# Cross-attention and sparse FFN: normed attention tiles without the turn back, with reciprocal norms spread over channels by DMA

## The reference, cut to what matters

```
def attention(q, k, v, ...):             # q = layernorm(x); k = v = ctx; per batch 64 channels x 512 positions
    qh, kh, vh = (W @ t split into 8 heads of 64 for W, t in ...)
    qh = softmax(qh, axis=channel) * SCALE;  kh = softmax(kh, axis=position)
    context = einsum('bhdn,bhen->bhde', kh, vh)
    out = einsum('bhde,bhdn->bhen', context, qh)          # then Wo @ out + bo: b x 64 x 512
    norm = max(sqrt(sum(out * out, axis=channel)), 1e-12) # one norm for each batch and position
    return out / norm * g * sqrt(64)

def ffn(x, c1_w, c2_w, w1, w2t):         # rows of 512, 1,792 = 56 blocks of 32 inner units
    idx = argmax of (x @ c1_w.T @ c2_w.T) in each block   # one unit in each block survives
    h = relu(w1[idx] . x);   return h @ w2t[idx]

x = x + attention(layernorm(x), ctx, ctx, ...)            # x, ctx: 32 x 64 x 512 float32
x = x + ffn(layernorm(x), ...)
```

## Time and profile before

| | |
|---|---|
| median of 3 runs | 748.57 us (748.07 to 752.73) |
| profiled execution | 750.29 us, of which the span 748.2 us |
| mean granted TensorE clock | 0.995 of full |
| DVE busy | 622.1 us (83%) |
| ACT busy | 400.9 us (54%) |
| POOL busy | 481.9 us (64%) |

### The profile page before, as it was taken

How to read it: one execution, slowest core, us unless ns; L and a number is a source line. 1 busy time by engine, 2 the same in 40 slices (tenths; PEclk the granted TensorE clock), 3 DMA queues, 4 the chain that set the end, 5 groups by cost and what they waited for, 6 DMA issues and landing times.

```text
span 748.2 us, 14582 instructions
## 1 busy us (share of the span) xinstructions
PE 737.2 (99%) x5210; PEld 563.3 (75%) x5210; DVE 622.1 (83%) x910; ACT 400.9 (54%) x773; POOL 481.9 (64%) x517
## 2 busy tenths in 40 slices
PE   8999999999999999999998999999999999999998
PEld 6566566566566566575667989898898989989896
DVE  6999999999999999999977677787877878777652
ACT  5899999999999999999830211111111111111110
POOL 2889999999988888687566263644535355263420
PEclk9999999999999999999998999999999999999999
DMA  6233434434433333231212113130130302111011
GB/s 169 71 85 101 127 103 107 126 98 113 120 91 89 96 93 91 71 86 43 78 29 64 38 24 105 21 106 20 25 105 20 106 19 75 52 24 50 20 52 34
DMA packets 66376, 55.23 MB, mean 74 GB/s; under 512 B 40704, under 2 KB 49536, under 8 KB 66304
## 3 DMA queue, kind: packets, MB, share of 16 engines
q1 hardware_dynamic: 65568, 53.44, 26.7%
q10 hardware_dynamic: 736, 0.85, 0.5%
HBM read 38.52 MB, written 8.39 MB: 63 GB/s over the span
## 4 chain that ended last, share of the span: by engine, by line
PE 90%; POOL 3%; SPq 2%; DVE 2%; ACT 2%; issue 1%; DMA 1%; POOLq 0%; DVEq 0%
PE slot L1106 20%; PE po L1234 14%; PE po L1124 11%; PE turn L1124 11%; PE turn L1219 8%; PE turn L1202 7%; PE slot L1260 6%; PE slot L1274 6%; PE po L1245 2%; SPq L275 2%; PE slot L1088 2%; POOL Q L532 2%; PE turn L1056 1%; PE turn L1065 1%; PE turn L1076 1%
## 5 line engine op out<-in xcount | busy, mean ns | idle before, releaser
L532 POOL TENSOR_TENSOR Q<-Q,qrec 128x1024 f32<-128x1024 f32 x64 | 121.2, 1905 | 33.8 <-DVE qrec L770 33.8
L422 POOL TENSOR_TENSOR E<-E,rank 128x512 bf16<-128x512 bf16 (+1 forms) x64 | 71.0, 1110 | 110.8 <-DVE E L618 109.8
L1237 PE MATMUL po<-QT,G 128*64 128x512 f32 x256 | 116.9, 599 | 0.0
L1234 PE MATMUL po<-E,ctxT 128*64 128x512 f32 x256 | 116.9, 599 | 0.0
L936 ACT ACTIVATE E<-slot,neg_kmax 128x512 f32<-128x512 f32 x128 | 86.4, 686 | 10.4 <-DVE neg_kmax L756 10.2
L722 DVE TENSOR_REDUCE qmax<-slot 128x16 f32<-128x1024 f32 x64 | 75.3, 1217 | 12.5 <-PE slot L1274 12.5
L1234 PEld LDWEIGHTS po<-E,ctxT 128*64 128x64 f32 x256 | 32.3, 136 | 65.0 <-issue 57.6
L435 POOL TENSOR_TENSOR behind<-E,first 128x512 bf16<-128x512 bf16 (+1 forms) x64 | 60.3, 943 | 31.7 <-DVE first L626 31.5
L762 DVE TENSOR_REDUCE qsum<-Q 128x16 f32<-128x1024 f32 x64 | 77.2, 1207 | 1.6 <-ACT Q L925 1.6
L756 DVE TENSOR_REDUCE neg_kmax<-slot 128x2 f32<-128x1024 f32 x64 | 76.3, 1193 | 0.6 <-PE slot L1260 0.2
L944 ACT ACTIVATE E<-turn 128x512 f32<-128x512 f32 x128 | 75.1, 613 | 3.1 <-PE turn L1202 2.1
(11 more groups left out here) (184 smaller groups left out, 1956.8 us busy)
## 6 DMA issues: line engine op xcount, KB each, us to landing
c_in<-in_ctx SPq DMA_DIRECT2D x64, 128.0 KB, 2.7
x_in<-in_x SPq DMA_DIRECT2D x64, 128.0 KB, 2.6
stage<-in_ffn_w SPq DMA_DIRECT2D x32, 225.0 KB, 2.6
out<-E SPq DMA_DIRECT2D x16, 256.0 KB, 2.3
ctxT<-in_ctxT SPq DMA_DIRECT2D x31, 128.0 KB, 2.1
attn_out<-po_sb SPq DMA_DIRECT2D x31, 128.0 KB, 2.3
attn<-attn_out SPq DMA_DIRECT2D x9, 256.0 KB, 3.7
E<-attn_out SPq DMA_DIRECT2D x7, 256.0 KB, 4.3
```

The lines of the kernel that those rows point to most:

```text
L532: nc.gpsimd.tensor_tensor(half, half, qrec[1 - par][:, s, :].unsqueeze(2).broadcast_to([P, HALF, D]), ALU.mult).then_inc(q_scaled, 1)
L1234: nc.tensor.matmul(po[0:C, :], ctxT[1 - par][:, m, :], E[1 - par][:, :, m * P:(m + 1) * P], start=(m == 0), stop=(m == NT - 1)).then_inc(p ...
L1237: nc.tensor.matmul(po[C:P, :], G[:, m, :], QT[m][:], start=(m == 0), stop=(m == HT - 1)).then_inc(out_mm, 1)
```

## The change

The attention tile is turned as before, but only to get the norms. ACT squares it in place in PSUM (`square`), and DVE's `norms` sums there. POOL inverts the norms of a pair of tiles in one pow over 16 columns (8 for tiles 0 and 1). PE turns these columns into rows: one transpose, `turn_factors`, in place of eight. ACT copies the 16 rows of 128 to SBUF (`keep_rows`), stores them to a new DRAM tensor `factors`, waits, and loads each batch's 512 factors back over 64 partitions (`exchange`: one store, four loads, on ACT's own queue; for tiles 0 and 1 on SP's). `scale` then multiplies the unturned tile by the spread factors, both in SBUF, and `residual` reads the tile from SBUF and not from a PSUM bank.

Orders change on every engine. `turn_attn`, `square` and `norms` of a pair stand one duo earlier (behind `down(d, 3)`); `turn_factors` stands behind `hide(d, 1)`. For tiles 0 and 1 norms sit in steps 24 and 27, scale (POOL) and residual in 26 and 29, moments in 28 and 30, and normalize is POOL's. SP loads the second attention tile of a pair after `added` and not after `attn_turned`.

```diff
+TURNS = (B - 8, B - 5)
...
-        norm, inv = ([sb(f"{n}{i}", [P, 2 * NT]) for i in range(2)] for n in ("norm", "inv"))
+        inv_rows = sb("inv_rows", [4 * NT, P])
+        norm, inv = (sb(n, [P, 2, 2 * NT]) for n in ("norm", "inv"))
...
-        attn = [attn0, E[0][:, 0, :]]
-        x2 = [x20, stage[1][:], E[0][:, 2, :], E[0][:, 3, :], po_sb[0][:], po_sb[1][:]]
-        works, turned_attns = [stage[0][:], work1[:]], [x_in[0][:], E[0][:, 1, :]]
-        attn_of = lambda a: attn0 if a < 2 else attn[a % 2]
-        work_of = lambda a: works[0] if a < 2 else works[a % 2]
-        square_of = lambda a: stage[1][:] if a == 1 else work_of(a)
-        turned_of = lambda a: (stage[1][:], attn0)[a] if a < 2 else turned_attns[a % 2]
+        attn = [stage[1][:], E[0][:, 0, :]]
+        x2 = [x20, attn0, E[0][:, 2, :], E[0][:, 3, :], po_sb[0][:], po_sb[1][:]]
+        works = [stage[0][:], work1[:]]
+        attn_of = lambda a: (attn0, stage[0][:])[a] if a < 2 else attn[a % 2]
+        work_of = lambda a: (stage[1][:], stage[0][:])[a] if a < 2 else works[a % 2]
+        spread_of = lambda a: (stage[1][:], attn0)[a] if a < 2 else (x_in[0][:], E[0][:, 1, :])[a % 2]
...
+        over_channels = lambda a, b: factors[a, b:b + 1].broadcast_to([C, N])
+        rows_of = lambda f: f.rearrange("b (t n) -> (b t) n", n=P)
+        by_pair = lambda ap: ap.rearrange("p (t b c) -> p t b c", b=2, c=C)
+        by_factor = lambda ap: ap.rearrange("p (b t) -> p t b", b=2)
+        inverted = lambda a: a + 1 if a < 2 else 2 + a // 2
...
+                def store_factor(a):
+                    sp.wait_ge(rows_kept, a + 1)
+                    sp.dma_start(rows_of(factors[a]), inv_rows[0:2 * NT, :]).then_inc(first_stored, 16)
+
+                def load_factor(a):
+                    sp.wait_ge(first_stored, 16 * (a + 1))
+                    for b in range(2):
+                        sp.dma_start(spread_of(a)[b * C:(b + 1) * C, :], over_channels(a, b)).then_inc(spread_in[a], 16)
...
-                    if known == 24:
+                    if known == TURNS[0] - 2:
...
-                            sp.wait_ge(attn_turned, a - 1)
+                            sp.wait_ge(added, a - 1)
...
+                def normalize(a):
+                    pool.wait_ge(x2_rstd, a + 1)
+                    nc.gpsimd.tensor_scalar(work_of(a), x2[a % 6], moments2[a][:, 0:1], rstd2[a][:], ALU.subtract,
+                                            ALU.mult).then_inc(x2_normed, 1)
+
+                def invert(a, w):
+                    pool.wait_ge(norm_max, a + w)
+                    if a > 1:
+                        pool.wait_ge(inv_turned, a // 2 + 1)
+                    nc.gpsimd.tensor_tensor(inv[:, a % 2:a % 2 + w], norm[:, a % 2:a % 2 + w],
+                                            neg_half[:].unsqueeze(2).broadcast_to([P, w, 2 * NT]),
                                             ALU.pow).then_inc(norm_inv, 1)
 
-                def scale_kept(a):
-                    pool.wait_ge(norm_inv, a + 1)
-                    pool.wait_ge(attn_kept, a + 1)
-                    nc.gpsimd.tensor_tensor(by_batch(turned_of(a)), by_batch(turned_of(a)),
-                                            inv[a % 2][:].unsqueeze(2).broadcast_to([P, 2 * NT, C]),
-                                            ALU.mult).then_inc(scaled, 1)
+                def scale(a):
+                    pool.wait_ge(spread_in[a], 32)
+                    nc.gpsimd.tensor_tensor(attn_of(a), attn_of(a), spread_of(a), ALU.mult).then_inc(scaled, 1)
...
-                    rank_mask(d, 3)
-                    select(d, 2)
-                    rank_mask(d, 4)
                     select(d, 3)
                     if not last:
-                        invert(2 * d + 2)
+                        invert(2 * d + 2, 2)
...
                     rank_mask(d, 0)
                     rank_mask(d, 1)
                     select(d, 0)
+                    rank_mask(d, 2)
                     select(d, 1)
-                    rank_mask(d, 2)
+                    rank_mask(d, 3)
+                    select(d, 2)
+                    rank_mask(d, 4)
...
-                def norms(a):
+                def norms(a, bank):
                     t = a % 2
                     dve.wait_ge(squared, a + 1)
                     if later(a - 1):
-                        dve.wait_ge(norm_inv, a - 1)
-                    nc.vector.tensor_reduce(norm[t][:], by_batch(square_of(a)), AX.X, ALU.add).then_inc(norm_sum, 1)
+                        dve.wait_ge(norm_inv, inverted(a - 2))
+                    nc.vector.tensor_reduce(by_factor(norm[:, t]), by_pair(bank[:]), AX.X, ALU.add).then_inc(norm_sum, 1)
                     dve.wait_ge(norm_sum, a + 1)
-                    nc.vector.tensor_scalar(norm[t][:], norm[t][:], NORM_EPS * NORM_EPS, None, ALU.max).then_inc(norm_max, 1)
+                    nc.vector.tensor_scalar(norm[:, t], norm[:, t], NORM_EPS * NORM_EPS, None, ALU.max).then_inc(norm_max, 1)
 
                 def scale(a):
-                    t = a % 2
-                    dve.wait_ge(norm_inv, a + 1)
-                    dve.wait_ge(attn_back, max(a - 1, 2))
-                    nc.vector.tensor_tensor(by_batch(turned_of(a)), by_batch(pre[t][:]),
-                                            inv[t][:].unsqueeze(2).broadcast_to([P, 2 * NT, C]), ALU.mult).then_inc(scaled, 1)
-
-                def residual(a, bank):
-                    t, r = a % 2, x2[a % 6]
-                    dve.wait_ge(attn_back, a + 1)
+                    dve.wait_ge(spread_in[a % 2], 32 * (a // 2 + 1))
+                    nc.vector.tensor_tensor(attn_of(a), attn_of(a), spread_of(a), ALU.mult).then_inc(scaled, 1)
+
+                def residual(a):
+                    r = x2[a % 6]
+                    dve.wait_ge(scaled, a + 1)
                     dve.wait_ge(gain_done, 1)
                     dve.wait_ge(xr_loaded[a % 4], 16 * (a // 4 + 1))
-                    nc.vector.scalar_tensor_tensor(r, bank[:], gain8[:, 0:1], r, ALU.mult, ALU.add).then_inc(added, 1)
+                    nc.vector.scalar_tensor_tensor(r, attn_of(a), gain8[:, 0:1], r, ALU.mult, ALU.add).then_inc(added, 1)
+
+                def moments_of(a):
...
+                    if later(q - 1):
+                        dve.wait_ge(hT_lo_done, q - 1)
...
-                    if d:
-                        first_max(d, 3)
+                    first_max(d, 3)
                     h_low(d, 0)
-                    if not last:
-                        norms(a)
                     first_max(d, 4)
                     block_max(d, 5)
-                    if not last:
-                        norms(a + 1)
-                        scale(a)
                     first_max(d, 5)
                     if d:
                         result_of(2 * d - 2)
                         result_of(2 * d - 1)
                     gate(d, 1)
-                    if not last:
-                        scale(a + 1)
                     block_max(d, 6)
                     h_low(d, 1)
-                    if not last:
-                        residual(a, pre[0])
                     gate(d, 2)
+                    if not last:
+                        for t in range(2):
+                            scale(a + t)
+                            residual(a + t)
+                            moments_of(a + t)
+                        normalize(a)
                     first_max(d, 6)
                     if not last:
-                        residual(a + 1, pre[1])
-                    h_low(d, 2)
+                        normalize(a + 1)
                     block_max(d, 7)
-                    if not last:
-                        normalize(a)
-                        normalize(a + 1)
-                    first_max(d, 7)
                     if not last:
                         xT_rest(a, pre[0])
                         xT_rest(a + 1, pre[1])
+                    h_low(d, 2)
+                    first_max(d, 7)
                     gate(d, 3)
+                    gate(d, 4)
+                    if not last:
+                        z_low(d + 1)
                     h_low(d, 3)
-                    gate(d, 4)
-                    if not last:
-                        z_low(d + 1)
-                    h_low(d, 4)
                     if not last:
                         block_max(d + 1, 0)
                         block_max(d + 1, 1)
                         first_max(d + 1, 0)
+                    h_low(d, 4)
+                    if not last:
                         block_max(d + 1, 2)
                         first_max(d + 1, 1)
+                        block_max(d + 1, 3)
                     gate(d, 5)
+                    if not last:
+                        first_max(d + 1, 2)
+                    gate(d, 6)
+                    if not last:
+                        block_max(d + 1, 4)
+                    if d + 2 < DUOS:
+                        norms(a + 2, pre[0])
                     h_low(d, 5)
```

(51 more changed lines are left out.)

126 lines of the change are left out of this document (62 added, 64 removed).

## The result

The changed kernel takes 743.69 us (median of 6 runs, 743.16 to 745.32) against 749.10 us for the kernel before (6 runs, 748.07 to 752.73): a ratio of 0.9926, 95% interval 0.9909 to 0.9942. Another five runs of it beside eleven of the kernel before gave 743.71 against 749.47, ratio 0.9929 (0.9917 to 0.9941). So it is faster, by 5.4 to 5.8 us or 0.7%: within 1%, inside the range of 738.5 to 748.0, and some 2.7 us above the 741.0 of the forecast. The profiled execution took 745.32 us with a span of 743.5 (before: 750.29 and 748.2).

What follows compares the result with a forecast made beforehand. TensorE (PE), busy 99% of the span, was taken as the bound; 4.0 (duos) + 2.8 (first duo) + 0.8 (attention) = 7.6 us gave 741.0 us. Summed terms ranged 739.0 to 743.5, the stated range 738.5 to 748.0.

Steps and rivals of the forecast that it cites:

- Part 1: Duos 1 to 6: eight transposes off PE, one added, net 0.67 us per duo, 4.0 us in all.
- The slack of 0.8 on DVE's chain: In each duo normalize(a+1) ends at 20.0 and PE wants it at 20.8 us, so PE need not wait.
- The first rival: Factors arrive late, so scale, DVE's queue and PE wait in each duo; up to 754 us, chance 0.12.
- the second, the port: DVE waits for POOL's SBUF port, four instructions a duo, each up to 0.65 us longer; taken at 747, chance 0.10.
- Part 2: First duo: PE leaves turn_x(3) at 409.2 instead of 411.98, gain 2.8 us.
- The stop at turn_factors: First duo: PE waits 2.1 us for POOL's power of sixteen columns, or 0.9 if it costs as little as eight.
- shorter than the 2.54 after which the clock was seen to fall: First duo: the new 2.1 us stop should leave PE's clock at full speed; if it falls, gain 1.2.
- Part 3: Attention steps 24 to 31: costs over plain steps fall from 3.9 to 3.0 to 3.4 us, gain taken as 0.8.
- the two residuals (0.75) by 0.15 each: Attention steps: each residual takes 0.75 us on DVE and exceeds the step's spare time by 0.15.
- The rule weighed: Scale and residual, now with both inputs in SBUF, and POOL's SBUF-reading instructions exclude each other; whichever starts second waits.
- the change gives only the PE work: First-duo stops return with the clock's fall and attention gains nothing: 4.0 + 0.7, 743.9 us, chance 0.08.

Runs made afterwards that it cites:

- turn_twice: Changed kernel with the eight transposes of turn_x done twice in duos 1 to 6, writing the same values: 748.87 us.
- store_twice: Changed kernel with the store of the factors sent twice, one behind the other, in duos 1 to 6: 746.67 us.
- first_split: Changed kernel; first duo: POOL's select(0,3) and power ahead of rank_mask(0,4), first_max(0,3) earlier, SP issues mask copies for gate(0,1) first: 744.93 us.
- again: The changed kernel run and profiled a second time, unedited, beside the experiments: 743.71 us, profile span 742.2.
- residual_beside: Changed kernel with residual(0) moved one step on, behind invert_q(0), where POOL starts a scaling of 1.9 us: 743.28 us in one run.
- first_ahead: Third edit of the first duo's order: first_split, with DVE's scale, residual and moments of tile 2 ahead of gate(0,2), normalize(3) ahead of first_max(0,6): 742.26 us.
- residual_late: Changed kernel with only residual(0) and residual(1) moved within their attention steps, to where POOL is idle: 743.51 us.

## Why the prediction was right or wrong, point by point

- **Part 1, PE's work per duo (4.0 us): right.** turn_x to turn_x is 43.91 to 44.04 us in four of the five pitches from duo 1 to duo 6, and 44.18 in the fifth, where 43.9 to 44.0 was named; the stretch behind the first duo shrank by 3.7. The missing 0.3 us lie behind PE's last matmul, whose start is 744.54 before and 739.56 after: from there to the end of the span it is 3.7 us before and 3.9 after. Up to that matmul PE gained the full 4.0. turn_twice gives the same price from the other side: 5.2 us for six duos of eight transposes.
- **The slack of 0.8 on DVE's chain: right within 0.2 in four duos of six** (0.65 in duos 2, 3, 4 and 6), and gone in duos 1 and 5 (0.05). store_twice bears this out: 1.4 us of delay cost 0.2 to 0.5 in those four, and 0.8 and 1.4 in the other two. Two terms inside it were wrong and cancelled, which was luck: the store lands in 1.4 and not 2.5, and the loads in 3.6 and not 2.6. The first rival, the late exchange, did come in duo 1 (scale waited 0.82 us), where the slack just took it. So did a little of the second, the port: scale(a) took 0.91 to 1.06 us in five of the seven duos and rank_mask(6) beside it 1.54 instead of 1.16, where the prediction had POOL's mask over before scale starts.
- **Part 2, the first duo (2.8 us): the number right (2.7), its working half so.** The stop at turn_factors came as forecast (2.39 against 2.1); it was longer because the power took 3.38 us and not 2.9, and 2.94 is what it took in first_split, where h_low(0,0) did not start ahead of it. The step that failed is the clock: "shorter than the 2.54 after which the clock was seen to fall" took one observed stop for a bound, and the clock fell behind a stop of 2.39, 0.9 us after PE had resumed. For that case the prediction had a gain of 1.2, and the gain was 2.7 all the same. The fall lost 1.7 us, half of the 3.4 of before, and these went where PE would have waited for normalize(3) anyway; only 0.41 of that wait was left. That this cost nothing on balance is luck; the one run of the changed kernel with a mean clock of 1.000 took 743.16 us, and the lowest of the other five, at 0.998, only 0.44 more. gate(0,1) was well placed: 399.83 less the 1.8 by which the first profile's step 31 is late gives 398.0, forecast 398.3.
- **Part 3, attention (0.8 us): wrong, it gave -0.3 to -0.6.** The step that failed is "the two residuals (0.75) by 0.15 each". The prediction had weighed the port rule and looked for the hit in the duos, and had taken 0.75 for the attention steps, where POOL was scaling Q and splitting x at that moment. They took 2.17 and 1.59 (again: 2.48 and 1.55), which makes step 26 12.82 us long. With the residuals out of POOL's way the eight steps come to 93.3, so 3.1 us over plain ones, inside the 3.0 to 3.4 that had been summed. The norms (0.6 in step 24, 0.5 in step 27) and scale's 1.27 us were as reckoned.
- **The rule weighed.** By the Trainium skill ("SBUF — State Buffer", who interferes with whom) a VectorE instruction with two SBUF inputs and a GpSimd instruction that reads SBUF exclude each other, and the one issued first keeps the port for its whole length. The traces agree three times: 0.75 became 2.17 and 1.59, and in residual_beside it was POOL that waited (2.26 for 1.90). One row does not fit: in first_split h_low(0,0) started 0.4 us before the end of POOL's power and took its plain 0.69 us. What was missing was not the rule but the place.
- **The sum.** 7.6 was forecast against the profiled execution of before; the two profiles of after give 4.7 and 6.0. Of the 1.6 that even the better one misses, 1.4 are attention and 0.3 the end behind PE's last matmul. By the medians the gain is 5.4 to 5.8: the kernel before also has runs in which its clock was granted 0.998 on average, 748.2 to 749.5 us, while the profiled execution at 750.29 is of those at 0.995. So part of the 3.4 us of half clock that the sum took as given was probably there only in some runs; this is inferred from the mean clocks, no second profile of before shows it. 743.69 lies 0.2 above the range of 739.0 to 743.5 that the prediction had summed from its terms, and next to its rival "the change gives only the PE work" (743.9). That nearness is chance: attention gave nothing, as in the rival, but the first duo gave 2.7 and not 0.7.

## What to carry to other kernels

Work taken from the engine that bounds was worth its length here within 0.1 us a duo, and could be priced by putting it back. A wait taken away in a ring of engines is worth only the distance to the next one: list who is late next, what lies queued behind it and which transfers the earlier start will meet before moving anything; here the third edit was the first to pay. When two profiles are compared, count from a common event and not from the start of the program. Where an instruction's inputs go from PSUM to SBUF on VectorE, look at what GpSimd runs at that very place, and use one of its idle gaps.

## What the runs showed of the hardware that was not expected

- The clock fell to half behind single stops of 2.31, 2.34, 2.39 and 3.83 us, and in first_split behind stops of 1.35 and 1.34 with 0.66 us of work between; it stayed at full speed in first_ahead with stops of 1.0, 1.0 and 0.6. Each of these falls lost 1.7 us of full speed, the one behind the 3.24 of before 3.4.
- At the program's start the same code had the clock at 1.00 in one profile and at 0.58 over 4 us in another, which made 1.7 us of difference by step 23 (3.1 in the profile of residual_late).
- A store of 8 KB from SBUF to DRAM on ScalarE's queue landed in 1.4 us; loads that spread one row of 512 over 64 partitions took 0.5 to 1.3 us to issue and 2.8 to 5.5 us to land.
- A transposing copy of the masks cost SP's queue about 1.23 us of issue, back to back, and landed 2.3 us behind it in the first duo of the changed kernel.
- GpSimd's power of sixteen columns took 2.94 us in first_split and 3.35 in the median of the changed kernel, that of eight 1.66, that of one 0.55.
